# Fixed stack rows filled by DMA, a shifted pass over 66 rows, and a later split of the wide weights

## The chip, the cores and the metric

The kernel runs on one core of a Trainium2 chip. The metric is the device time of one execution in microseconds: 266.58 us before, the median of three runs (266.46 to 270.88). Five engines work beside each other: PE (matrix products, PEld is its weight load), DVE (vector), ACT (activations, copies), POOL (GpSimd) and SP, which here only issues DMAs. DMAs that SP issues go through one queue (q1), those that ACT issues through another (q10). Engines meet only at semaphores.

## The reference

One transformer layer in float32: 4 sequences ("batches") of 256 tokens, width 256, 16 heads of 16, feed-forward width 1024.

```python
x = x + attn(layernorm(x))
x = x + ffn(layernorm(x))

# attn, per batch and head
q, k, v = h @ Wq.T, h @ Wk.T, h @ Wv.T          # rotary embedding on q and k
kf, qf  = elu(k) + 1, elu(q) + 1
lin     = (qf @ (kf.T @ v)) / (qf . sum(kf))    # linear attention
att     = softmax(q @ k.T / 4) @ v
out     = (sigmoid(gate) * lin + (1 - sigmoid(gate)) * att) @ Wo.T

# ffn
out = fwht(silu(h @ W1.T) * (h @ W3.T)) @ W2.T  # fwht: Walsh-Hadamard over 1024
```

## The kernel before

Float32 values are carried as a high and a low part (`_hi`, `_lo`), each rounded to the format that TensorE takes at full rate; a product is the sum of three products of parts. The Hadamard transform is folded into W2 once.

**The stacks.** `q_stack` and `k_stack` are [128, 16 heads, 256 tokens]. For each head, rows 0 to 47 hold q parts (hi, lo, hi) and k parts (hi, hi, lo), 16 rows each, so that one product over the rows gives the three-part product. `scores` (L897) multiplies rows 0 to 63 and DVE takes row maxima (`row_maxima`, L624). The negated maxima then come by DMA into rows 64 and 65 of `q_stack` (`MAXROW` is 64), where `k_stack` holds ones, and `shifted_scores` (L913) multiplies all 128 rows: it gives the score less its row maximum, and ACT takes the exponential (L364). Every other row has to be zero. Rows 0 to 47 are gathered from `parts`, a tensor in DRAM: SP writes the parts there (`write_parts`, L260, four DMAs of 256 KB a batch) and reads them back head by head (`load_stacks`, L271, for each half `c` of the heads six DMAs of 128 KB, each of 16 rows with 8 pieces of 1 KB).

**The order of the work** is written out by hand, one program for each engine. Before the rounds stands a head for batch 0: layer norm (`ln_statistics`, POOL's `rstd` L496, `ln_normalise` L607), transposes on PE (L857), `evac_hT` on ACT (L316), `low_hT` on DVE (L612), the q and k products (L844 to L846), rotary products and sums (L635, L640), the split into parts (`split_parts` L322 on ACT, `first_low_part` L645 on DVE), `write_parts`, `load_stacks`, and the first scores. Beside it ACT and POOL split the wide weights W1 and W3 (`wide_raw`, 128x2048 each) into `w13_hi` (`split_wide`, L408) and `w13_lo` (L539), which the feed-forward reads first in round 1. After the head, round r works on attention of batch r, on projections of batch r+1 and on feed-forward of batches r-1 and r-2.

**Fixed rows.** POOL sets all of `q_stack` to zero (L487) first of all, then computes `rstd` of batch 0, then sets all of `k_stack` to zero (L531) and its rows 64 and 65 to one (L533), and counts `stack_zero` to 2, on which the first `load_stacks` waits.

**SP's order** in the head: x of batch 0, Wq, Wk, x of batch 1, W1, W3; then, once the narrow weights are split, W2 (L248, into the same buffer), x of batches 2 and 3, and Wo (L253, four DMAs of 16 rows); then the four writes of `parts`, and the twelve loads.

Of the kernel before, what the change touches and what calls it, by code (L numbers as in the profile page):

```python
# [48 lines left out]
P = 128  # L49
# [35 lines left out]
def build(nc, x, wqT, wkT, wvT, woT, gate, w1T, w3T, w2T, const, out):  # L85
    with ExitStack() as ctx:
# [7 lines left out]
        def bank(name):  # L94
# [31 lines left out]
        w2_lo = sb("w2_lo", [P, FC, D], F32R)  # L126
        wo = sb("wo", [P, NG, D])
        stats = sb("stats", [P, TT, 6])
        mv = sb("mv", [P, TT, 2])
# [38 lines left out]
        w13_in = [sem("w1_in"), sem("w3_in")]  # L168
        (const_in, w2_in, wo_in, gate_in, mhalf_set, wo_zero, stack_zero, k_zero, v_const, mem_zero, wqkv_hi_s, wqkv_lo_s, w13_hi_s, w1_lo_s, w3_lo_s,
         had_ps, had_sb, fly, w2_hi_s, w2_lo_s, gate_exp, gate_s) = [sem(n) for n in (  # L170
             "const_in w2_in wo_in gate_in mhalf_set wo_zero stack_zero k_zero v_const mem_zero wqkv_hi_s wqkv_lo_s w13_hi_s w1_lo_s w3_lo_s "
             "had_ps had_sb fly w2_hi_s w2_lo_s gate_exp gate_s").split()]
# [63 lines left out]
        def _(sp):  # L236
# [7 lines left out]
            for m, w in enumerate((w1T, w3T)):  # L244
                sp.dma_start(wide_raw[:, m], w.rearrange("(c p) n -> p c n", p=P)).then_inc(w13_in[m], 16)
            sp.wait_ge(wqkv_hi_s, 3)
            sp.wait_ge(wqkv_lo_s, 3)
# [14 lines left out]
            def load_stacks(b, c):  # L262

                sp.wait_ge(parts_out[c], 32 * (b + 1))
                if b == 0:
                    sp.wait_ge(stack_zero, 2)
                else:
                    sp.wait_ge(exp_ps, NH * (b - 1) + HH * (c + 1))
                for m, stack, slots in ((0, q_stack, (0, 1, 0)), (1, k_stack, (0, 0, 1))):
                    for s, half in enumerate(slots):  # L270
                        sp.dma_start(stack[HD * s:HD * s + HD, HH * c:HH * c + HH, :].bitcast(F32),  # L271
                                     parts[b, half, c, m].rearrange("(h d) n -> d h n", d=HD)).then_inc(stack_in[c], 16)
# [29 lines left out]
        def _(act):  # L302
# [116 lines left out]
            evac_hT(0)  # L419
            for m in range(2):  # L420
                split_wide(m)
            for r in ROUNDS:
# [17 lines left out]
                if r >= 0 and has(r + 1):  # L440
                    evac_v(r + 1)
                if r < 0:
                    exp_elu(0)
                    evac_hT(1)
                    evac_hadamard(0)
                    evac_kfT(0)
                    evac_hadamard(1)
                    continue
# [36 lines left out]
        def _(pool):  # L485
            pool.memset(mhalf[:], -0.5).then_inc(mhalf_set, 1)
            pool.memset(q_stack[:].bitcast(F32), 0.0).then_inc(stack_zero, 1)  # L487

# [41 lines left out]
            ln_power(0)  # L530
            pool.memset(k_stack[:].bitcast(F32), 0.0).then_inc(k_zero, 1)  # L531
            pool.wait_ge(k_zero, 1)
            pool.memset(k_stack[MAXROW:MAXROW + 2].bitcast(F32), 1.0).then_inc(stack_zero, 1)  # L533
            pool.wait_ge(stack_zero, 2)
            ln_power(1)
            pool.memset(wo[:], 0.0).then_inc(wo_zero, 1)
            for m, done in enumerate((w1_lo_s, w3_lo_s)):
                pool.wait_ge(w13_hi_s, m + 1)
                pool.tensor_tensor(w13_lo[:, m], wide_raw[:, m], w13_hi[:, m].bitcast(F32), ALU.subtract).then_inc(done, 1)  # L539
# [293 lines left out]
        def _(pe):  # L833
# [74 lines left out]
            def shifted_scores(b, h):  # L908
# [3 lines left out]
                for tt in range(TT):  # L912
                    mm = pe.matmul(bank[:, tt, :], k_stack[:, h, tt * P:tt * P + P], q_stack[:, h, :],  # L913
                                   start=True, stop=True)
# [231 lines left out]
```

## Time and profile before

| What | us |
|---|---|
| Median of three runs | 266.58 |
| Lowest, highest | 266.46, 270.88 |
| Span of the profiled execution, first to last instruction | 262.9 |
| Own device time of the profiled execution | not given by the page |
| Busy: PE, PEld, DVE, ACT, POOL | 215.3, 171.7, 175.3, 97.8, 95.5 |
| First scores of batch 0 start at | 41.87 |

Instruction times are counted from the start of the span. A timeline row gives the start, the length, the engine, the source line and the operation; with xcount over 1 the length is that of the merged run from the first start to the last end. "[a <-b]" is the idle time of the engine before the row and what ended it. The chain of waits is followed back from the last instruction; "issue" in it is time in which the engine named next waited for nothing that the profile shows. A window's DMA share is the mean busy share of the 16 DMA engines.

### The profile page before, as it was taken

Reading aid. Unit: us, or ns where it says so; the run is one execution under the profiler, and the core shown is the slowest. Engines: PE = TensorE matmul, PEld = TensorE weight load, DVE = VectorE, ACT = ScalarE, POOL = GpSimd, SP = SyncE. Lnnn points to the kernel's source line nnn. Section 1 sums busy time; section 2 is a strip of 40 time slices with the busy share of each in tenths; the row PEclk is TensorE's granted clock in tenths of the full one; section 3 lists DMA queues with packets and bytes.
Section 4 is the critical chain, followed back from the end, with each engine's and each line's share of the span. In section 5 each row is a group of like instructions: output and inputs, shape, how many; then the busy total and the mean of one; then the engine's idle time right before and its main releaser. Section 6 shows DMA issues by size and latency. Waiting matters only on the chain.

```text
span 262.9 us, 4040 instructions
## 1 busy us (share of the span) xinstructions
PE 215.3 (82%) x1444; PEld 171.7 (65%) x1444; DVE 175.3 (67%) x340; ACT 97.8 (37%) x196; POOL 95.5 (36%) x73
## 2 busy tenths in 40 slices
PE   0073086887969869999998999999999999986894
PEld 0072056665548558896786788977767896765893
DVE  6958842688886984719869927375997734774532
ACT  2261040043963021468701312688011466612331
POOL 7929400189044364233502461243011224201332
PEclk9999557997999967999999569999999999999999
DMA  7928299031287013005560130026800010000101
GB/s 224 356 59 223 99 177 118 6 134 31 46 101 97 0 40 122 5 1 87 87 70 1 40 122 1 5 59 94 133 0 0 5 42 0 4 0 1 42 1 40
DMA packets 16916, 17.57 MB, mean 67 GB/s; under 512 B 1664, under 2 KB 16256, under 8 KB 16896
## 3 DMA queue, kind: packets, MB, share of 16 engines
q1 hardware_dynamic: 16144, 16.59, 30.1%
q10 hardware_dynamic: 752, 0.73, 0.9%
q8 instruction: 11, 0.18, 0.4%
q14 instruction: 9, 0.07, 0.1%
HBM read 11.93 MB, written 5.24 MB: 65 GB/s over the span
## 4 chain that ended last, share of the span: by engine, by line
PE 48%; issue 21%; DVE 13%; POOL 8%; DMA 6%; SPq 2%; ACT 2%; POOLq 0%; DVEq 0%; ACTq 0%
PE score_bank L897 7%; DMA k_stack<-parts 5%; PE exp_bank L1004 5%; PE score_bank L1004 4%; PE exp_bank L913 4%; DVE rowmax L624 4%; POOL hid_lo L522 4%; PE down_bank L1026 4%; DVE xn L607 4%; PE misc_bank L844 3%; PE misc_bank L963 3%; PE misc_bank L845 2%; PE misc_bank L846 2%; DVE prod L635 2%; PE pv_bank L930 2%
## 5 line engine op out<-in xcount | busy, mean ns | idle before, releaser
L624 DVE TENSOR_REDUCE rowmax<-score_bank 128x2 f32<-128x512 f32 x64 | 43.2, 685 | 30.2 <-PE score_bank L897 30.1
L522 POOL TENSOR_TENSOR hid_lo<-wide_raw,hid_hi 128x256 fp32r<-128x256 f32 x32 | 24.8, 774 | 80.1 <-ACT hid_hi L397 76.6
L364 ACT ACTIVATE prob<-exp_bank 128x512 f32<-128x512 f32 x64 | 37.8, 600 | 14.1 <-PE exp_bank L913 13.8
L897 PE MATMUL score_bank<-k_stack,q_stack 64*128 64x256 f32 x128 | 31.5, 339 | 11.5 <-DVE rowmax L624 7.2
L897 PEld LDWEIGHTS score_bank<-k_stack,q_stack 64*128 64x128 f32 x128 | 19.7, 198 | 23.8 <-DVE rowmax L624 9.1
L913 PE MATMUL exp_bank<-q_stack,k_stack 128*128 128x256 f32 x128 | 28.6, 307 | 1.2 <-ACT prob L364 1.1
L913 PEld LDWEIGHTS exp_bank<-q_stack,k_stack 128*128 128x128 f32 x128 | 19.2, 188 | 12.7 <-issue 8.2
L503 POOL TENSOR_TENSOR roped<-prod 128x512 f32<-128x512 f32 x6 | 7.6, 1269 | 44.8 <-DVE prod L635 44.8
L857 PE MATMUL misc_bank<-cst,xn 128*128 128x128 f32 x16 | 3.4, 352 | 24.2 <-DVE xn L607 24.2
L734 DVE SCALAR_TENSOR_TENSOR wide_raw<-wide_raw,score_bank 128x256 f32<-128x256 f32 x16 | 6.7, 417 | 23.3 <-ACT wide_raw L391 23.3
L1004 PE MATMUL exp_bank<-h2T_hi,w_hi 128*128 128x256 f32 x64 | 19.4, 324 | 0.0
L1026 PE MATMUL down_bank<-w_hi,hid_hi 128*128 128x256 f32 x64 | 17.8, 300 | 1.5 <-ACT hid_hi L397 1.4
L857 PEld LDWEIGHTS misc_bank<-cst,xn 128*128 128x128 f32 x16 | 2.4, 179 | 24.4 <-issue 13.1
L607 DVE TENSOR_SCALAR xn<-xs,mv,rstd 128x256 f32<-128x256 f32 x16 | 12.3, 808 | 8.0 <-POOL rstd L496 7.7
L982 PE MATMUL pv_bank<-wo,att 128*128 128x256 f32 x64 | 16.7, 389 | 1.0 <-DVE att L719 1.0
L1004 PE MATMUL exp_bank<-h2T_hi,w_lo 128*128 128x256 f32 x64 | 17.1, 288 | 0.0
L1004 PE MATMUL score_bank<-h2T_hi,w_hi 128*128 128x256 f32 x64 | 17.0, 289 | 0.0
L1026 PE MATMUL down_bank<-w_lo,hid_hi 128*128 128x256 f32 x64 | 16.7, 282 | 0.0
L1004 PE MATMUL score_bank<-h2T_hi,w_lo 128*128 128x256 f32 x64 | 16.4, 279 | 0.0
L391 ACT ACTIVATE wide_raw<-exp_bank 128x256 f32<-128x256 f32 x16 | 6.2, 384 | 26.3 <-PE exp_bank L1008 24.3
L376 ACT ACTIVATE xs<-pv_bank 128x512 f32<-128x512 f32 x4 | 2.4, 598 | 35.8 <-DVE stats L588 35.8
L930 PE MATMUL pv_bank<-prob,v_strips 128*32 128x256 f32 x192 | 15.3, 391 | 0.1
(116 smaller groups left out, 548.1 us busy)
## 6 DMA issues: line engine op xcount, KB each, us to landing
q_stack<-parts SPq DMA_DIRECT2D x24, 128.0 KB, 4.0
k_stack<-parts SPq DMA_DIRECT2D x24, 128.0 KB, 5.3
parts<-part_hi SPq DMA_DIRECT2D x8, 256.0 KB, 2.2
parts<-part_lo SPq DMA_DIRECT2D x8, 256.0 KB, 3.1
xs<-in_x SPq DMA_DIRECT2D x4, 256.0 KB, 6.5
wide_raw<-in_w1T SPq DMA_DIRECT2D x1, 1024.0 KB, 8.0
wide_raw<-in_w3T SPq DMA_DIRECT2D x1, 1024.0 KB, 10.0
narrow_raw<-in_w2T SPq DMA_DIRECT2D x1, 1024.0 KB, 6.1
```

The lines of the kernel that those rows point to most:

```text
L364: act.activation(prob[:, h % 8], exp_bank[h % 2][:], ACT.Exp, scale=SCALE).then_inc(prob_s, 1)
L522: pool.tensor_tensor(hid_lo[:, n % 3, :], ffn_work[n % 3], hid_hi[:, n % 3, :].bitcast(F32), ALU.subtract).then_inc(hid_lo_s, 1)
L607: dve.tensor_scalar(xn[:, tt, :], xs[:, b, tt, :], mv[:, tt, 0:1], rstd[:, tt:tt + 1], ALU.subtract, ALU.mult).then_inc(ln_xn, 1)
L624: dve.tensor_reduce(rowmax[:, h, :], score_bank[h % 2][:], AX.X, ALU.max).then_inc(rowmax_s, 1)
L844: pe.matmul(out_ap, lhs[0], rhs[0], start=start, stop=False, **kw)
L897: mm = pe.matmul(bank[:, tt, :], q_stack[0:MAXROW, h, tt * P:tt * P + P], k_stack[0:MAXROW, h, :], start=True, stop=True)
L913: mm = pe.matmul(bank[:, tt, :], k_stack[:, h, tt * P:tt * P + P], q_stack[:, h, :], start=True, stop=True)
L930: mm = pe.matmul(bank[STRIP * j:STRIP * j + STRIP, half, :], v_strips[b % 2][:, tt, h, :], prob[:, h % 8, tt, :], start=(tt == 0), stop=(t ...
L963: mm = pe.matmul(bank[:, u, :], mem[:, c, 4 * u:4 * u + 4, :].rearrange("p h e -> p (h e)"), feat[:, c, 0, :], start=True, stop=True)
L982: mm = pe.matmul(bank[:, tt, :], att[:, g, tt * P:tt * P + P], wo[:, g, :], start=False, stop=(g == NG - 1), skip_group_check=True)
L1004: pe.matmul(bank[:, m, :], w[:, m, k, cols], h2T_hi[:, k, :], start=(k == 0 and w is w13_hi), stop=False)
L1026: pe.matmul(bank[:, tt, :], hid_hi[:, n % 3, tt * P:tt * P + P], w[:, c, :], start=(c == 0 and tt == 0 and w is w2_hi), stop=False, skip_g ...
```

## The change

Three parts. (1) POOL no longer writes the stacks: it writes a tile `fill` [128, 2, 256], zeros and ones, and SP issues three DMAs that copy rows of it to the fixed rows: `q_stack` rows 48 to 65 and `k_stack` rows 48 to 63 from zeros, `k_stack` rows 64 and 65 from ones. They stand after W3 and ahead of W2. Rows 66 to 127 are not written any more. (2) `shifted_scores` multiplies rows 0 to 65. (3) ACT's two `split_wide` stand after `split_parts` of batch 0, and POOL's `w13_lo` waits for `feat_s`, the features of batch 0.

```diff
+        fill = sb("fill", [P, 2, S])
...
+            sp.wait_ge(fill_set, 2)
+            for rows, value in ((q_stack[3 * HD:MAXROW + 2], 0), (k_stack[3 * HD:MAXROW], 0), (k_stack[MAXROW:MAXROW + 2], 1)):
+                n = rows.shape[0]
+                sp.dma_start(rows.bitcast(F32), fill[0:n, value, :].unsqueeze(1).broadcast_to([n, NH, S])).then_inc(stack_zero, 16)
             sp.wait_ge(wqkv_hi_s, 3)
...
-                    sp.wait_ge(stack_zero, 2)
+                    sp.wait_ge(stack_zero, 48)
...
             evac_hT(0)
-            for m in range(2):
-                split_wide(m)
...
                 if r < 0:
+                    split_wide(0)
                     exp_elu(0)
                     evac_hT(1)
+                    split_wide(1)
                     evac_hadamard(0)
...
-            pool.memset(q_stack[:].bitcast(F32), 0.0).then_inc(stack_zero, 1)
+            for k in range(2):
+                pool.memset(fill[:, k, :], float(k)).then_inc(fill_set, 1)
...
             ln_power(0)
-            pool.memset(k_stack[:].bitcast(F32), 0.0).then_inc(k_zero, 1)
-            pool.wait_ge(k_zero, 1)
-            pool.memset(k_stack[MAXROW:MAXROW + 2].bitcast(F32), 1.0).then_inc(stack_zero, 1)
-            pool.wait_ge(stack_zero, 2)
             ln_power(1)
             pool.memset(wo[:], 0.0).then_inc(wo_zero, 1)
+            pool.wait_ge(feat_s, 1)
             for m, done in enumerate((w1_lo_s, w3_lo_s)):
...
-                    mm = pe.matmul(bank[:, tt, :], k_stack[:, h, tt * P:tt * P + P], q_stack[:, h, :],
+                    mm = pe.matmul(bank[:, tt, :], k_stack[0:MAXROW + 2, h, tt * P:tt * P + P], q_stack[0:MAXROW + 2, h, :],
```

On SP, from W3's load to the first load of the stacks, the order before was (`narrow_raw<-in_w2T` is W2, `parts<-` are the writes of the parts):

```order
L245 DMA wide_raw<-in_w3T 128x2x1024
L248 DMA narrow_raw<-in_w2T 128x8x256
L250 DMA xs<-in_x 128x2x256 x2
L253 DMA wo<-in_woT 16x4x256 x4
L260 DMA parts<-part_hi 128x2x256
```

and is now:

```order
L246 DMA wide_raw<-in_w3T 128x2x1024
L250 DMA q_stack<-fill 18x16x256
L250 DMA k_stack<-fill 16x16x256
L250 DMA k_stack<-fill 2x16x256
L253 DMA narrow_raw<-in_w2T 128x8x256
L255 DMA xs<-in_x 128x2x256 x2
L258 DMA wo<-in_woT 16x4x256 x4
L265 DMA parts<-part_hi 128x2x256
```

Three DMAs with 576 pieces of 1 KB stand ahead of W2 in the queue; nothing else of SP's order moved.

On ACT, from the split of the narrow weights to the first `evac_hadamard`, the order before was (`w_hi<-wide_raw` is `split_wide`, `prod<-prod` the exponential for the features):

```order
L310 ACTIVATE wqkv_hi<-narrow_raw 128x512 x3
L316 ACTIVATE hT_hi<-misc_bank 128x512
L408 ACTIVATE w_hi<-wide_raw 128x2048 x2
L330 ACTIVATE v_strips<-down_bank 128x32x16
L322 ACTIVATE part_hi<-roped 128x512 x2
L335 ACTIVATE prod<-prod 128x1024
L316 ACTIVATE hT_hi<-misc_bank 128x512
L413 ACTIVATE narrow_raw<-exp_bank 128x512
```

and is now:

```order
L315 ACTIVATE wqkv_hi<-narrow_raw 128x512 x3
L321 ACTIVATE hT_hi<-misc_bank 128x512
L335 ACTIVATE v_strips<-down_bank 128x32x16
L327 ACTIVATE part_hi<-roped 128x512 x2
L413 ACTIVATE w_hi<-wide_raw 128x2048
L340 ACTIVATE prod<-prod 128x1024
L321 ACTIVATE hT_hi<-misc_bank 128x512
L413 ACTIVATE w_hi<-wide_raw 128x2048
L418 ACTIVATE narrow_raw<-exp_bank 128x512
```

The first half of the wide split now stands ahead of the exponential, the second behind the second `hT_hi`.

On POOL, between the first `rstd` and the rotary sums, it was:

```order
L487 MEMSET q_stack 128x4096
L496 ISA
L496 TENSOR_TENSOR rstd<-var_eps,mhalf 128x2
L531 MEMSET k_stack 128x4096
L533 MEMSET k_stack 2x4096
L496 TENSOR_TENSOR rstd<-var_eps,mhalf 128x2
L536 MEMSET wo 128x1024
L539 TENSOR_TENSOR w_lo<-wide_raw,w_hi 128x2048 x2
```

and is now:

```order
L493 MEMSET fill 128x256 x2
L502 ISA
L502 TENSOR_TENSOR rstd<-var_eps,mhalf 128x2 x2
L538 MEMSET wo 128x1024
L542 TENSOR_TENSOR w_lo<-wide_raw,w_hi 128x2048 x2
```

The three large memsets are gone, and `w_lo` keeps its place but has the new wait in front.

## Rows read from the trace of the kernel before

**Rows 1.** The page's first line and its chain, shares of the span by engine

```profile
span 262.9 us, 4040 instructions
...
PE 48%; issue 21%; DVE 13%; POOL 8%; DMA 6%; SPq 2%; ACT 2%; POOLq 0%; DVEq 0%; ACTq 0%
```

**Rows 2.** Chain of waits in order of time: start us, us, what

```profile
21.86 2.78 DVE roped L640
...
31.55 0.70 DVE part_lo L645
...
35.12 6.71 DMA k_stack<-parts
...
41.87 0.74 PE score_bank L897 x4
```

**Rows 3.** Timeline of POOL: start us, us, engine, line, out<-in, xcount

```profile
5.69 3.51 POOL L531 MEMSET k_stack<- 128x4096 f32 x1
9.26 3.54 POOL L533 MEMSET k_stack<- 2x4096 f32 x1
...
19.50 9.48 POOL L539 TENSOR_TENSOR w_lo<-wide_raw,w_hi 128x2048 fp32r<-128x2048 f32 x2
...
72.59 3.27 POOL L528 TENSOR_TENSOR wide_raw<-wide_raw,narrow_raw 128x1024 f32<-128x1024 f32 x1 [6.46 <-DVE narrow_raw L707]
```

**Rows 4.** Timeline of DVE, same columns

```profile
5.79 7.16 DVE L607 TENSOR_SCALAR xn<-xs,mv,rstd 128x256 f32<-128x256 f32 x2 [0.88 <-POOL rstd L496]
...
25.32 4.21 DVE L645 TENSOR_TENSOR part_lo<-roped,part_hi 128x512 fp32r<-128x512 f32 x1
...
30.17 0.69 DVE L640 TENSOR_TENSOR roped<-prod 128x512 f32<-128x512 f32 x1
...
32.16 0.73 DVE L607 TENSOR_SCALAR xn<-xs,mv,rstd 128x256 f32<-128x256 f32 x2
...
34.62 1.23 DVE L656 SCALAR_TENSOR_TENSOR feat<-roped,prod 128x1024 f32<-128x1024 f32 x1 [1.12 <-ACT prod L335]
...
75.18 0.71 DVE L702 TENSOR_TENSOR ginv<-inv,gate 128x16 f32<-128x16 f32 x1
```

**Rows 5.** Timeline of ACT, same columns

```profile
7.32 1.15 ACT L310 ACTIVATE wqkv_hi<-narrow_raw 128x512 fp32r<-128x512 f32 x2 [0.54 <-DMA narrow_raw<-in_wkT]
14.22 0.60 ACT L316 ACTIVATE hT_hi<-misc_bank 128x512 fp32r<-128x512 f32 x1 [5.75 <-PE misc_bank L857]
14.71 3.70 ACT L408 ACTIVATE w_hi<-wide_raw 128x2048 fp32r<-128x2048 f32 x2
```

**Rows 6.** Timeline of SP's DMA issues, same columns

```profile
3.25 0.80 SPq L245 DMA_DIRECT2D wide_raw<-in_w3T  x1
16.83 0.37 SPq L248 DMA_DIRECT2D narrow_raw<-in_w2T  x1
...
25.32 0.39 SPq L260 DMA_DIRECT2D parts<-part_hi  x1
```

**Rows 7.** Windows: stretch, length, busy by engine, granted PE clock, DMA share, GB/s

```profile
10.00:12.40 2.40, 0.00 (x0) 0.00 (x0) 2.40 (x1) 0.00 (x0) 2.40 (x1) 1.00 0.97 387
12.60:17.00 4.40, 2.45 (x10) 2.11 (x11) 3.09 (x7) 2.78 (x3) 0.20 (x1) 1.00 0.00 1
17.80:26.20 8.40, 4.03 (x28) 3.83 (x27) 5.56 (x6) 1.84 (x3) 8.25 (x4) 1.00 0.81 219
26.20:27.40 1.20, 0.00 (x0) 0.00 (x0) 1.20 (x1) 0.00 (x0) 1.20 (x1) 0.54 0.63 219
34.40:46.20 11.80, 8.50 (x36) 6.68 (x34) 4.04 (x9) 2.46 (x5) 0.00 (x0) 0.64 1.12 127
23.20:26.20 3.00, 0.00 (x0) 0.00 (x0) 2.91 (x3) 0.63 (x1) 3.00 (x2) 1.00 0.57 76
```

**Rows 8.** Timeline of PE, the two score passes, same columns as in 3

```profile
57.03 0.73 PE L897 MATMUL score_bank<-k_stack,q_stack 64*128 64x256 f32 x4
...
72.48 0.74 PE L913 MATMUL exp_bank<-q_stack,k_stack 128*128 128x256 f32 x4
```

More of the change, by code:

```diff
@@ L168, in build @@
         w13_in = [sem("w1_in"), sem("w3_in")]
-        (const_in, w2_in, wo_in, gate_in, mhalf_set, wo_zero, stack_zero, k_zero, v_const, mem_zero, wqkv_hi_s, wqkv_lo_s, w13_hi_s, w1_lo_s, w3_lo_s,
+        (const_in, w2_in, wo_in, gate_in, mhalf_set, wo_zero, stack_zero, fill_set, v_const, mem_zero, wqkv_hi_s, wqkv_lo_s, w13_hi_s, w1_lo_s, w3_lo_s,
          had_ps, had_sb, fly, w2_hi_s, w2_lo_s, gate_exp, gate_s) = [sem(n) for n in (
-             "const_in w2_in wo_in gate_in mhalf_set wo_zero stack_zero k_zero v_const mem_zero wqkv_hi_s wqkv_lo_s w13_hi_s w1_lo_s w3_lo_s "
+             "const_in w2_in wo_in gate_in mhalf_set wo_zero stack_zero fill_set v_const mem_zero wqkv_hi_s wqkv_lo_s w13_hi_s w1_lo_s w3_lo_s "
              "had_ps had_sb fly w2_hi_s w2_lo_s gate_exp gate_s").split()]
```

## The prediction

> **What bounds the kernel now.** I read the page first. Its chain is PE for 48% of the span and "issue" for 21% [rows 1]: over most of the run PE is the bound, and the change takes no work from PE there. So I went to the stretch that the change edits, the head up to the first scores, by the chain in order of time. The head is one serial chain: layer norm, transposes, the q and k products, the rotary sums (the first takes 2.78 us), the last `part_lo` at 31.55, the loads of the stacks (the last of the first half issued at 35.12 and landed 6.71 later), and scores at 41.87 [rows 2]. What the head loses, every later round gets back one for one, since nothing behind it waits for anything but the work ahead of it.
>
> Two pieces of it are not work. On DVE two `xn` take 7.16 us where the same two take 0.73 at 32.16 [rows 4]; during the 7.16 POOL clears `k_stack`, 5.69 to 12.80 [rows 3]. And `part_lo` takes 4.21 at 25.32 where such an instruction takes 0.69 to 0.70, the rotary sum 2.78 where the next takes 0.69 [rows 2, 4]; each ends about when one of POOL's two `w_lo` ends (24.2 and 29.0) [rows 3]. DVE is held by POOL's instruction in both places.
>
> **The compute side of the head.** *First piece.* Without the memsets `xn` ends at 5.79 + 0.73 = 6.5, and the transposes after it (1.1) at 7.7. Now ACT's narrow splits are late next: they end at 7.32 + 1.15 = 8.5 [rows 5]. `hT_hi` starts there and not at 14.22: 5.7 us earlier. DVE's `wqkv_lo` fits between. *Second piece.* Without `w_lo` beside them the sum saves 2.78 - 0.69 = 2.1 and the low part 4.21 - 0.69 = 3.5: 5.6 us. The last `part_lo` would start at 31.55 - 5.7 - 5.6 = 20.2 and end at 20.9, 11.3 us earlier. *ACT's moved work.* Each `split_wide` takes 1.9 [rows 5]. The first fits between the second `part_hi` (ends 20.2) and the exponential (22.2), so it costs nothing; the second delays only `kfT`, which is wanted when the scores are. *POOL's moved work.* `w_lo` starts when `feat` ends, 34.62 + 1.23 - 11.3 = 24.6 [rows 4], and takes 9.48 [rows 3]: to 34.1. DVE has two instructions of four columns for the gate in its way. A small one, 16 columns at 75.18, takes 0.71, as long as 512 columns do elsewhere, and ends with POOL's instruction at 75.9 [rows 3, 4]. So I let both wait, the second to 34.1, and the first row maximum of batch 0 can't start before 34.3. POOL's next work (from 51.5) is late enough. *66 rows.* Four matmuls over 64 rows take 0.73, four over 128 rows 0.74 [rows 8]. 66 lies between: zero, at most 0.01 for four, 0.3 us over 128. *`fill`.* Two memsets of 256 columns at 3.51 / 4096 per column [rows 3]: 0.4 us, long done when SP has issued W3 at 4.05 [rows 6].
>
> **The queue side.** This decides. The parts may be ready at 20.9, but their writes stand in SP's queue behind everything issued earlier. Before, the engines were busy to 12.4, idle from 12.6 to 17.0, since W2 was issued only at 16.83, and worked on W2, x and Wo from 17.8 to 26.2; the first write moved from 26.2 [rows 6, 7]. So the queue was clear just when the first parts came. Now:
>
> - W3 is through at 12.5, as before. The fills follow at once: 18, 16 and 2 rows of 16 KB, 590 KB. No fill is in the trace. The nearest row is the stack loads, 1 KB pieces into 16 partitions of the same tiles: 127 GB/s [rows 7], which gives 4.7 us. The ends are the full-width write, 1.20 x 0.63 = 0.76 us for 262 KB, or 1.7 us, and the Wo loads, 76 GB/s, or 7.8 us [rows 7]. I take 4.7, since tile, width and piece are the same: done at 17.2. They fall into the hole that the queue had.
> - W2, x and Wo are now waiting in line. By rate it is 1.57 MB at 387 GB/s, 4.1 us, and Wo's 3.0: 7.1. As traced it is 8.4 [rows 7]. I take 7.7: to 24.9.
> - The four writes of parts, 4 x 0.76 = 3.0: to 27.9. SP needs only the first two landed (26.5) to issue the loads, and first bytes follow an issue by some 0.9 us (25.32 to 26.2, [rows 6, 7]), so the loads follow at 28.0.
> - Before, loads moved from 34.4, and the first half was complete at 41.82 [rows 2, 7]: 7.4 us. Now it is complete at 35.4.
>
> That is 41.8 - 35.4 = 6.4 us, against 11.3 that the engines could give; 34.3 on DVE covers it by a microsecond. After the first scores nothing differs. The granted clock in 34.4 to 46.2 was 0.64 [rows 7], so these products already ran mostly at 1.2 GHz; PE idles longer ahead of them now, and I count nothing either way. The sum against the profiled span is 262.9 - 6.4 = 256.5. The median lies 3.7 above that span; the page gives no own time for the profiled execution, and I let the 3.7 stand: **260.2 us**.
>
> A rule of the Trainium skill bears on the fills. "DMA: Bandwidth & Descriptors", section "Why a DMA increments its semaphore by 16 and not by 1", says that a DMA is spread over the largest number of engines up to 16 that divides its slowest dimension on both sides: 9 engines for 18 rows, 2 for 2 rows. No row of the trace shows such a shape. By it some engines carry more than the mean, which is the second rival below, and the sum would be 263.4 in place of 260.2.
>
> **Rivals.** One: *the fills are cheap.* SBUF to SBUF at the rate of the full-width write, 1.7 us. Then the loads are complete at 32.4 and the gain is 9.4: 257.2. For it: nothing in DRAM is read. Against it: all writes go to 18 partitions, and both traced transfers into 16 partitions were slow. DVE's 34.3 doesn't take it back: PE has products of batch 1 to do after the first two scores, and needs the first maximum only for the third score.
>
> Two: *an uneven split.* If each piece takes an engine what a load's piece took (11.8 us for 96 pieces an engine, 123 ns, [rows 7]) and the 18 rows go to 9 engines, the fullest engine has 32 + 16 + 16 pieces: 7.9 us in place of 4.7. The gain is 3.2: 263.4. Against it: fewer engines on the same rows would disturb each other less than 16 do.
>
> Three, the slower side: *the fills block the queue.* If 18 rows go to two engines only, these have 144 + 16 + 16 pieces, 21.6 us at 123 ns; W2, Wo and the parts wait behind them from 12.5 to 34.1. The first half is then complete at 52.3, 10.5 us later than before: 277.1. It decides against the change once the fills take over 4.7 + 6.4 = 11.1 us. For it: they stand ahead of all that the head still needs. Against it: 16-row loads show no such concentration.
>
> Four: *the engines' gain isn't there*, DVE being slow for another cause than POOL. Then parts come at the old pace and nearly nothing is gained; the pairs 7.16 / 0.73 and 4.21 / 0.69 speak against it. About 266.
>
> **Numbers.** Forecast 0.50 (its own range 258.5 to 262.5: the 7.1 or 8.4 for W2 to Wo, and fills of 3.5 to 6.5 us), cheap fills 0.20, uneven split 0.22, blocked queue 0.05, no gain 0.03. The range 256.8 to 264.5 takes in the first three but their tails. A change under 2%, 5.3 us, counts as none: the border is 261.2. Of the forecast's half some 0.35 lies under it, with the cheap fills 0.55 faster; the rest of the forecast, the uneven split and no gain make 0.40; slower 0.05.
>
> **What would show it.** In the new profile the two first `xn` together under 0.8 us, `hT_hi` of batch 0 at 8.5, no `part_lo` over 0.8, the last one ended by 21. Then the queue: the DMA engines busy without a hole from 12.5 to 40, the fills landed near 17, the writes of parts landing 5 us or more after their issue, first scores near 35.5. If the writes land 2 us after their issue, the queue was not the bound and rival one holds or better; if the fills land at 20, rival two; beyond 23, rival three. I am wrong altogether if the first scores start at 35.5 and the span shrinks by much less than 6: then something behind the head took it back, and I have named nothing for that.

## The result, and the profile after the change

The changed kernel took **269.23 us** (median of 20 runs, 266.88 to 274.26), the kernel before 266.41 beside it (20 runs). By these medians it is slower by 1.1%, or 2.8 us, where 260.2 us and faster were forecast. The executions of one kernel fall into shorter and longer ones, some 4 us apart (shown below); over the shorter ones alone the ratio is 1.0206, with a 95% interval of 1.016 to 1.0252. The sign is clear and the size is 1 to 2%; whether it passes 2% isn't settled.

The page of the kernel after, first line, granted clock in 40 slices, and shares of the chain (as [rows 1]):

```profile
span 265.7 us, 4043 instructions
...
PEclk9995575997555896899999999999999999999999
...
PE 51%; issue 18%; DMA 8%; POOL 7%; DVE 7%; SPq 5%; ACT 2%; POOLq 0%; DVEq 0%; ACTq 0%
```

The same line of the clock in the kernel before:

```profile
PEclk9999557997999967999999569999999999999999
```

The span grew from 262.9 to 265.7, and the slices 10 to 12, counted from 0 (66 to 86 us), are the place to look: three fives, where before has 9, 9 and 9.

**The engines did what was forecast.** DVE in the head (columns as in [rows 4]: start, us, engine and line, tiles, count, and in brackets the idle time before and who ended it):

```profile
5.66 0.74 DVE L610 TENSOR_SCALAR xn<-xs,mv,rstd 128x256 f32<-128x256 f32 x2 [0.88 <-POOL rstd L502]
...
17.04 0.69 DVE L648 TENSOR_TENSOR part_lo<-roped,part_hi 128x512 fp32r<-128x512 f32 x1
...
19.76 0.69 DVE L648 TENSOR_TENSOR part_lo<-roped,part_hi 128x512 fp32r<-128x512 f32 x1 [0.70 <-ACT part_hi L327]
...
24.57 4.09 DVE L750 TENSOR_SCALAR gsum<-gexp 128x4 f32<-128x4 f32 x1
...
28.90 4.22 DVE L754 TENSOR_SCALAR gate<-gate 128x4 f32<-128x4 f32 x1
41.21 1.29 DVE L627 TENSOR_REDUCE rowmax<-score_bank 128x2 f32<-128x512 f32 x2 [8.09 <-PE score_bank L900]
```

ACT and POOL there:

```profile
8.37 0.58 ACT L321 ACTIVATE hT_hi<-misc_bank 128x512 fp32r<-128x512 f32 x1
```

```profile
24.13 8.96 POOL L542 TENSOR_TENSOR w_lo<-wide_raw,w_hi 128x2048 fp32r<-128x2048 f32 x2 [10.50 <-DVE feat L659]
```

The two first `xn` take 0.74 us, `hT_hi` starts at 8.37 (forecast 8.5), no `part_lo` is over 0.69, the last ends at 20.45 (forecast 20.9), and the gate's four-column instructions are held for 4.1 and 4.2 us until `w_lo` is done at 33.1.

**The queue did not.** SP's issues, as [rows 6], and the chain of waits behind them:

```profile
3.80 1.01 SPq L250 DMA_DIRECT2D q_stack<-fill  x1
4.86 1.42 SPq L250 DMA_DIRECT2D k_stack<-fill  x2
...
11.41 8.03 SPq L255 DMA_DIRECT2D xs<-in_x  x2
19.48 2.94 SPq L258 DMA_DIRECT2D wo<-in_woT  x4
22.47 0.43 SPq L265 DMA_DIRECT2D parts<-part_hi  x1
...
25.52 1.36 SPq L265 DMA_DIRECT2D parts<-part_lo  x1
31.78 1.27 SPq L276 DMA_DIRECT2D q_stack<-parts  x3
```

```profile
22.95 8.81 DMA parts<-part_lo
34.03 6.30 DMA k_stack<-parts
40.38 1.22 PE score_bank L900 x4
```

The DMA engines and the clock in three stretches (as [rows 7]):

```profile
26.00:31.80 5.80, 3.76 (x11) 3.12 (x12) 5.73 (x3) 1.20 (x2) 5.80 (x2) 0.50 0.53 164
36.00:40.00 4.00, 0.00 (x0) 0.00 (x0) 0.00 (x0) 0.00 (x0) 0.00 (x0) 0.60 1.16 116
40.00:46.00 6.00, 5.62 (x24) 5.37 (x24) 1.80 (x4) 0.00 (x0) 0.00 (x0) 0.50 0.95 100
```

SP needed 8.03 us to issue two loads of x; before, the same row read 1.10 (at 17.24). The writes of parts, ready from 17.7, were issued at 22.47 and 22.95, and the first two had landed only at 31.76, 8.8 us after the second one's issue. In 26.0 to 31.8 the DMA engines were busy for a 0.53 share on average, against 1.13 in 12 to 24: at the end the landing waited for a remainder; which engines still carried it the window doesn't show.

The fills didn't follow W3, as forecast, but ran beside it. The view of DMAs (KB each, us from issue to landing) has for W3 and W2, now:

```profile
wide_raw<-in_w3T SPq DMA_DIRECT2D x1, 1024.0 KB, 15.5
narrow_raw<-in_w2T SPq DMA_DIRECT2D x1, 1024.0 KB, 17.0
```

and before:

```profile
wide_raw<-in_w3T SPq DMA_DIRECT2D x1, 1024.0 KB, 10.0
narrow_raw<-in_w2T SPq DMA_DIRECT2D x1, 1024.0 KB, 6.1
```

W3, issued ahead of the fills at 3.29, was complete at 18.8 in place of 13.2. The view gives no landing for the fills, but the trace keeps each time at which a DMA raised a semaphore, and on `stack_zero` the last of them is at 23.6 us: the fills were complete there, and not at 17.2.

The scores started at 40.38, 1.5 us earlier than before and 5 later than forecast. PE had then done nothing from 32.7 on, its clock stood at 0.50 (1.2 GHz) through 46, and of the 1.5 us only 0.25 were left at the next scores (46.20 against 46.45), behind the same products.

**Behind the head**, where "nothing differs" was written, PE in batch 0's shifted pass:

```profile
64.35 0.74 PE L916 MATMUL exp_bank<-q_stack,k_stack 66*128 66x256 f32 x4
...
67.86 1.08 PE L933 MATMUL pv_bank<-prob,v_strips 128*32 128x256 f32 x8
```

and before, where the lines are not among the rows above:

```profile
64.42 0.73 PE L913 MATMUL exp_bank<-q_stack,k_stack 128*128 128x256 f32 x4
...
67.72 0.64 PE L930 MATMUL pv_bank<-prob,v_strips 128*32 128x256 f32 x8
```

The first 66-row products at 64.35 take as long as 128-row ones. But from 68 on the same work takes nearly twice as long: `pv_bank`, whose shape the change doesn't touch, 1.08 in place of 0.64. The windows tell why. Before:

```profile
64.00:68.00 4.00, 3.27 (x22) 1.88 (x20) 3.39 (x6) 3.40 (x7) 2.12 (x2) 1.00 0.00 0
68.00:72.00 4.00, 3.99 (x42) 2.27 (x38) 3.69 (x6) 3.92 (x7) 0.00 (x0) 1.00 0.25 60
72.00:76.00 4.00, 3.47 (x33) 1.72 (x34) 3.86 (x7) 3.29 (x7) 3.27 (x1) 1.00 1.17 127
```

After:

```profile
64.00:68.00 4.00, 3.28 (x18) 1.91 (x20) 3.38 (x6) 3.29 (x7) 2.07 (x2) 0.93 0.00 0
68.00:72.00 4.00, 4.00 (x25) 2.15 (x23) 3.69 (x5) 2.66 (x4) 0.00 (x0) 0.50 0.00 0
72.00:76.00 4.00, 4.00 (x25) 1.93 (x24) 2.25 (x3) 2.22 (x5) 3.25 (x1) 0.50 0.97 137
```

In 68 to 72 PE is as busy (3.99 and 4.00 of 4 us), but it gets through 25 products in place of 42: the granted clock is 0.50 in place of 1.00, and it stays there up to 88.

A mark that all kernels have shows where time went: ACT's first instruction of the shifted pass of each batch (`nmT_hi`), and the steps from one to the next, in us. Each row is one profiled execution; the kernels are those of the next section, and "best" is the fastest of them by its median.

| kernel | first scores | batch 0's mark | to batch 1's | to 2's | to 3's | to the end |
|---|---|---|---|---|---|---|
| before | 41.87 | 61.31 | 47.5 | 53.9 | 44.7 | 55.4 |
| after | 40.38 | 61.24 | 54.1 | 50.1 | 44.8 | 55.5 |
| change repeated | 39.69 | 59.84 | 52.8 | 54.0 | 44.8 | 55.5 |
| before, 96 rows | 41.65 | 61.66 | 49.4 | 54.0 | 44.8 | 55.5 |
| before, 66 rows | 41.77 | 62.21 | 54.0 | 53.9 | 44.7 | 55.5 |
| late split | 36.30 | 59.26 | 48.8 | 52.5 | 44.7 | 56.9 |
| late split, 66 rows | 36.40 | 59.38 | 53.7 | 49.8 | 44.7 | 56.2 |
| change, 128 rows | 35.72 | 56.69 | 47.9 | 49.8 | 44.7 | 56.3 |
| best | 30.03 | 49.84 | 49.2 | 49.8 | 44.7 | 56.2 |
| best, 66 rows | 30.14 | 50.06 | 52.7 | 49.7 | 44.7 | 56.4 |

Against before, the profiled execution of the change has -0.1 at the first mark, +6.6 in the step behind it, -3.8 in the next and +0.1 at the end: +2.8, the whole of 265.7 - 262.9. The -3.8 is not the change's own: that step takes 49.7 to 50.2 or 53.9 to 54.0 in nearly every kernel, and the change has once the one and once the other.

### The profile page after: what moved, and what is told of

It reads as the page before. It is cut to its first block, busy times and chain, and to the rows that moved or that the text cites. A ratio compares the mean times of both kernels' runs of the same rounds, so it can differ in the third digit from the quotient of the medians.

```text
span 265.7 us, 4043 instructions
## 1 busy us (share of the span) xinstructions
PE 220.9 (83%) x1444; PEld 174.1 (66%) x1444; DVE 170.4 (64%) x340; ACT 98.0 (37%) x196; POOL 84.9 (32%) x72
## 4 chain that ended last, share of the span: by engine, by line
PE 51%; issue 18%; DMA 8%; POOL 7%; DVE 7%; SPq 5%; ACT 2%; POOLq 0%; DVEq 0%; ACTq 0%
PE score_bank L900 7%; PE exp_bank L916 6%; PE exp_bank L1007 4%; PE pv_bank L933 4%; PE score_bank L1007 4%; POOL hid_lo L528 4%; PE down_bank L1029 3%; DVE rowmax L627 3%; DMA parts<-part_lo 3%; PE misc_bank L966 3%; SPq L255 3%; PE misc_bank L847 3%; DMA k_stack<-parts 2%; DMA narrow_raw<-in_wkT 2%; PE misc_bank L956 2%
## 5 line engine op out<-in xcount | busy, mean ns | idle before, releaser
L528 POOL TENSOR_TENSOR hid_lo<-wide_raw,hid_hi 128x256 fp32r<-128x256 f32 x32 | 24.6, 770 | 76.6 <-ACT hid_hi L402 73.0
L916 PE MATMUL exp_bank<-q_stack,k_stack 66*128 66x256 f32 x128 | 31.3, 334 | 1.0 <-ACT prob L369 1.0
L916 PEld LDWEIGHTS exp_bank<-q_stack,k_stack 66*128 66x128 f32 x128 | 21.2, 209 | 14.8 <-issue 7.4
L933 PE MATMUL pv_bank<-prob,v_strips 128*32 128x256 f32 x192 | 18.0, 452 | 0.0
L985 PE MATMUL pv_bank<-wo,att 128*128 128x256 f32 x64 | 16.7, 389 | 1.0 <-DVE att L722 1.0
L1007 PE MATMUL exp_bank<-h2T_hi,w_lo 128*128 128x256 f32 x64 | 16.7, 284 | 0.0
L327 ACT ACTIVATE part_hi<-roped 128x512 fp32r<-128x512 f32 x8 | 5.0, 630 | 29.0 <-POOL roped L509 26.7
L502 POOL TENSOR_TENSOR rstd<-var_eps,mhalf 128x2 f32<-128x2 f32 x8 | 6.0, 756 | 28.1 <-DVE var_eps L600 27.9
L402 ACT ACTIVATE hid_hi<-wide_raw 128x256 fp32r<-128x256 f32 x32 | 13.3, 415 | 4.3 <-DVE wide_raw L740 4.0
```

The lines of the kernel that those rows point to most:

```text
L402: act.activation(hid_hi[:, n % 3, :], ffn_work[n % 3], ACT.Copy).then_inc(hid_hi_s, 1)
L528: pool.tensor_tensor(hid_lo[:, n % 3, :], ffn_work[n % 3], hid_hi[:, n % 3, :].bitcast(F32), ALU.subtract).then_inc(hid_lo_s, 1)
L916: mm = pe.matmul(bank[:, tt, :], k_stack[0:MAXROW + 2, h, tt * P:tt * P + P], q_stack[0:MAXROW + 2, h, :], start=True, stop=True)
L933: mm = pe.matmul(bank[STRIP * j:STRIP * j + STRIP, half, :], v_strips[b % 2][:, tt, h, :], prob[:, h % 8, tt, :], start=(tt == 0), stop=(t ...
L985: mm = pe.matmul(bank[:, tt, :], att[:, g, tt * P:tt * P + P], wo[:, g, :], start=False, stop=(g == NG - 1), skip_group_check=True)
L1007: pe.matmul(bank[:, m, :], w[:, m, k, cols], h2T_hi[:, k, :], start=(k == 0 and w is w13_hi), stop=False)
```

## The experiments

Ratios are to the kernel before beside it; intervals are 95%. "Median" is over all runs of that kernel, with the median of before in brackets. My theory after the result had two parts: 66 rows cost PE its clock in batch 0's shifted pass, and the fills cost the queue what the engines gained. The rivals were that one of them alone did it, or that the late split did.

### What each part does alone

**Only 66 rows**, and **96 rows**:

```diff
-mm = pe.matmul(bank[:, tt, :], k_stack[:, h, ...], q_stack[:, h, :], ...)
+mm = pe.matmul(bank[:, tt, :], k_stack[0:MAXROW + 2, h, ...], q_stack[0:MAXROW + 2, h, :], ...)   # rows66
+mm = pe.matmul(bank[:, tt, :], k_stack[0:MAXROW + 32, h, ...], q_stack[0:MAXROW + 32, h, :], ...)  # rows96
```

> The kernel before with one edit: the shifted pass multiplies rows 0 to 65 in place of all 128; the other rows are zero, so nothing is left out. Rows theory (the chip grants the lower clock in a stretch where PE multiplies 66 rows and has little else): in batch 0 the shifted pass, which has no feed-forward work beside it, runs at a granted clock near 0.5 from about 68 us on, the first scores of batch 1 come near 82 us in place of 78.25, and the time is 3 to 6 us above before. Timing theory (in the changed kernel the clock fell because the pass came in another phase after another head; the rows play no part): batch 0's pass keeps a clock of 1.0 as before and the time stays within 1 us of before.

> The kernel before with the shifted pass over rows 0 to 95. A dose test of the rows theory. If what counts is the number of rows fed to PE, 96 lies between 66 and 128: the clock falls for part of batch 0's pass or not at all, and the time is 0 to 4 us above before. Timing theory: as before, within 1 us.

66 rows: 1.0275 [1.0225, 1.0325], median 271.02 (265.4). 96 rows: 1.0058 [1.0001, 1.0116], median 267.59, 2.2 us over. Windows with 66 rows:

```profile
64.00:68.00 4.00, 3.72 (x12) 2.65 (x11) 3.39 (x6) 2.50 (x5) 3.04 (x2) 0.50 0.02 4
```

and with 96:

```profile
64.00:68.00 4.00, 3.54 (x14) 2.23 (x12) 3.39 (x6) 2.68 (x7) 2.17 (x2) 0.74 0.00 0
68.00:72.00 4.00, 3.99 (x38) 2.28 (x38) 3.70 (x6) 3.92 (x7) 0.00 (x0) 1.00 0.11 33
```

The head is unchanged in both (41.77 and 41.65). With 66 rows the clock is at 0.50 from 64 to 88 and batch 0's step takes 54.0 in place of 47.5; with 96 it is 0.74 in 64 to 68, 1.00 in 68 to 76 and 0.61 in 80 to 84, and the step takes 49.4. So the number of rows alone brings it about, without the fills and with the old order, and it is worth 5.6 us by the medians. The rows that are left out hold zeros: that they hold nothing does not make them worthless for the clock.

**Only the late split**, then **with 66 rows**:

```diff
 evac_hT(0)
-for m in range(2):
-    split_wide(m)
 ...
+    split_wide(0)
     exp_elu(0)
     evac_hT(1)
+    split_wide(1)
 ...
 pool.memset(wo[:], 0.0).then_inc(wo_zero, 1)
+pool.wait_ge(feat_s, 1)
```

> The kernel before with only the wide split moved late (ACT and POOL, as in the change); POOL's memsets and 128 rows stay. Each piece of the head on its own: the first xn still takes 7.2 us, part_lo and the rotary sum take 0.69 each, the last part_lo ends at 26.6. W2 is still issued at 16.8, so the queue is clear at 26.2 and the writes of the parts start there. First scores at 36 to 37.5 in place of 41.87, and the time 3 to 6 us under before. If only the sum of all parts brings anything (rival), the first scores stay above 40 and the time within 1 us of before.

> The kernel late_split (before with only the wide split moved late, 257.3) with the shifted pass over 66 rows and nothing else: all of the change but the fills. Rows theory: the granted clock is 0.5 through batch 0's shifted pass, and the time is 4 to 7 us over late_split: 261 to 264.5. What then lies between this and the changed kernel is the price of the fills in SP's queue, less the 6 us that POOL's memsets hold xn: 3 to 7 us. If rows play no part: 257 to 258.5.

Late split alone: **0.9689** [0.964, 0.9738], median 257.25 (265.51). With 66 rows: 1.0023 [0.9978, 1.0068], median 263.09 (264.72). The memsets still hold `xn` for 7.16 us, but parts are ready at 26.9 in place of 32.2, and the queue takes them at once: first scores 36.30, 5.6 earlier, just the 5.6 worked out for this piece. The time fell by 8.3 us, more than the 3 to 6 expected. 66 rows take 5.8 of the 8.3 us back. The profiled execution of the late split was its slowest (263.9 us, span 262.1), so its head is read from it and not its later steps. In the head it has 2.1 us at batch 0's mark; with a short step to batch 2's mark (4.1) that makes 6 of the 8.3 us, and where the rest comes from no trace of a typical run shows. The mark came 2.1 us earlier, and not 5.6. Two things stand between it and the scores: the clock was 0.50 from 48 to 64, with 66 rows too, where before had 1.00 up to 60, and the first maximum waits (below). How they share the 3.5 us isn't shown. DVE in the late split, the cover that I had at a microsecond:

```profile
35.39 4.24 DVE L752 TENSOR_SCALAR gate<-gate 128x4 f32<-128x4 f32 x1
39.54 1.27 DVE L625 TENSOR_REDUCE rowmax<-score_bank 128x2 f32<-128x512 f32 x2
```

Here the gate's wait does hold the first maximum: the scores are there at 36.30, the maximum starts at 39.54. What that costs this version wasn't tried.

**The change, with the wide split in its old place**, run twice, and **the change once more** beside it:

```diff
 evac_hT(0)
+for m in range(2):
+    split_wide(m)
 ...
-    split_wide(0)
     exp_elu(0)
     evac_hT(1)
-    split_wide(1)
 ...
-pool.wait_ge(feat_s, 1)
```

> The changed kernel with the wide split back in its old place: fills and 66 rows, without the third part. hT_hi is still early (8.4), ACT's two w_hi follow it at 13.3, when W3 has landed, so POOL's w_lo runs from about 15 to 25 and holds the rotary sums and low parts again: the last part_lo ends near 26 to 28. By then the queue, held by the 18-row fill, is nearly clear (31.8 for the first writes' landing in the changed kernel), so the head loses little against the changed kernel: first scores at 40 to 42.5 and time 268 to 272. If the late split is what costs in the change (rival), this kernel is 2 us and more faster than the change.

> The kernel fill_old_split (fills, 66 rows, wide split in its old place) beside the changed kernel on the same chip. Late split costs: 1.5% or more under the changed kernel, first scores no later than its. Chip and hour only: within 1% of it.

> The changed kernel once more, beside its relatives on one chip. It was 2.1% over before when measured alone; its relative with the old wide split (fill_old_split) was level with before on another chip. If the late split costs in the company of the fills, this kernel is 1.5% or more over that relative here too: 268 to 270 against 265 to 266.5. If the two differ by the chip and the hour only, both lie within 1% of each other.

Old place: 0.9984 [0.995, 1.0019] and 1.0111 [1.0038, 1.0185], medians 265.54 (266.11) and 265.77 (264.72). The change again: 1.0211 [1.0133, 1.0289], median 268.74. The first run's issues:

```profile
11.31 5.95 SPq L255 DMA_DIRECT2D xs<-in_x  x2
...
26.25 0.36 SPq L265 DMA_DIRECT2D parts<-part_lo  x1
31.46 1.27 SPq L276 DMA_DIRECT2D q_stack<-parts  x3
```

The parts are ready 5.8 us later than in the change (the last `part_lo` starts at 25.53, not 19.76), and yet the stack loads are issued at 31.46, not 31.78, and the scores start at 40.04, not 40.38. **Beside the fills the late split, worth 8 us by itself, gains nothing: the writes wait for the DMA engines and not for DVE.** In the second run of it the scores start at 37.99, against 39.69 in the repeated change. The expected 268 to 272 us did not come: by the medians the change is 3.7 and 3.0 us slower than this version, so that the rival, that the late split costs beside the fills, fits the first pair. In the second the ratios differ by 1.0%, between what either side had asked for, and their intervals overlap. The spans of its two profiled executions differ by 3.7 us: 1.4 at the first mark, -1.1 in the next step, 4.2 by a long step against a short one (see below) and -0.8 at the end. Whether the change has the long step more often isn't shown, and the cause stays open.

### The fills

**18 rows as 16 and 2**; then **16 rows only, and the ones of k behind Wo** (the two rows of q get the maximum later anyway; both kernels have 66 rows):

```diff
-for rows, value in ((q_stack[3 * HD:MAXROW + 2], 0), (k_stack[3 * HD:MAXROW], 0), (k_stack[MAXROW:MAXROW + 2], 1)):
+for rows, value in ((q_stack[3 * HD:MAXROW], 0), (q_stack[MAXROW:MAXROW + 2], 0), (k_stack[3 * HD:MAXROW], 0), (k_stack[MAXROW:MAXROW + 2], 1)):   # q16_2
+fill_rows(q_stack[3 * HD:MAXROW], 0)           # ones_late
+fill_rows(k_stack[3 * HD:MAXROW], 0)
 ... (W2, x, Wo)
+fill_rows(k_stack[MAXROW:MAXROW + 2], 1)
 ... (ahead of the first load of the stacks)
-sp.wait_ge(stack_zero, 48)
+sp.wait_ge(stack_zero, 64)                     # q16_2 only: four fills
```

> The changed kernel with one edit: the fill of the 18 rows of q_stack is issued as two DMAs, of 16 and of 2 rows. The bytes and the rows are the same, the shifted pass stays at 66 rows. Uneven split theory (18 rows are carried by fewer DMA engines, so those lag, hold SP's issue of x and the landing of everything behind): SP issues the two x loads in about 4 us in place of 8.03, the first scores come at 35.5 to 37 in place of 40.4, and the time is 2 to 5 us under the changed kernel, 264 to 267, with the clock still at 0.5 in batch 0's shifted pass. Bytes theory (590 KB into few rows take this long however they are cut): SP's issue still takes about 8 us, the first scores stay near 40.4 and the time near 269.

> The changed kernel with both odd shapes out of the way: q_stack gets only its 16 rows 48 to 63 (rows 64 and 65 are overwritten by the maxima anyway), and the 2 rows of ones go behind Wo. The shifted pass stays at 66 rows. This is the kernel after128 but for the number of rows and POOL's two memsets. Split theory: SP's two x issues take about 4 us, the first scores come at 35 to 36.5 (after128: 35.72; q fill in 16 + 2 rows: 37.91; change: 40.38). Rows theory: the granted clock is 0.5 through batch 0's shifted pass again, first scores of batch 1 near 77.5 to 79 in place of after128's 74.0, and the time is 3 to 7 us above the 257 of after128's undisturbed runs: 261 to 265. If the rows play no part, it equals after128 within 1 us.

Ratios 1.0032 [0.9999, 1.0065] and 1.0038 [0.9959, 1.0117], medians 266.56 (265.51) and 267.07 (266.11). SP with 16 and 2:

```profile
11.86 6.10 SPq L255 DMA_DIRECT2D xs<-in_x  x2
```

x takes 6.10 us to issue in place of 8.03, and with the ones late as well 4.08; first scores 37.91 and 37.76. Neither comes as early as expected (37 and 36.5 at the latest), and the second one's time is above its 261 to 265 us. One execution each can't give a price of the shape at the first scores either: with the fills of 18, 16 and 2 rows as they are, the same issue took 8.03 and 6.42 us in the change and 5.95 and 4.76 with the wide split in its old place, and the first scores came between 37.99 and 40.38. In time the shape does count: the change has 1.0206 and 1.0211, these two 1.0032 and 1.0038, and the intervals don't meet. By the medians that is some 2 us.

"DMA: Bandwidth & Descriptors" of the Trainium skill, section "Why a DMA increments its semaphore by 16 and not by 1", gives 18 rows 9 engines and 16 rows 16. The trace agrees. By that section a DMA on fewer than 16 engines raises its semaphore once for each of them and once, at its issue, for the rest, so 18, 16 and 2 rows make 10 + 16 + 3 = 29 increments. `stack_zero` has 29 in the change, two of them at 5.2 and 6.7 us, right behind the issues, and the other 27 from 16.7 on; it has 38 with rows of 16, 2, 16 and 2, and 35 with 16, 16 and 2.

**x and Wo behind the stack loads:**

```diff
-for b in range(2, NB): sp.dma_start(xs[:, b], ...)
-(the wait for wo_zero and the four Wo loads)
 ...
         load_stacks(r + 1, c)
+    if r < 0: (the same x and Wo loads)
```

> The changed kernel with the loads of x of batches 2 and 3 and of Wo moved on SP behind the loads of the stacks of batch 0 (66 rows as in the change). Queue theory (the head is bound by what stands in SP's queue ahead of the writes of the parts, and by SP being held while it issues them): x and Wo take some 4 to 5 us out of the line, the first scores come 4 to 6 us earlier, at 34.5 to 36.5 in place of 40.4, and the time falls by 3 to 6 us. Rival (the fills themselves or the loads' own rate hold the head): first scores stay within 1.5 us of 40.4 and the time within 1.5 us of the changed kernel.

0.9971 [0.9923, 1.002], median 263.93 (265.4). Parts are issued as soon as they are ready (17.31, the last at 20.75), the loads at 26.23, first scores 34.76. That is 7.1 us of head, yet at most 1% in time: in the profiled executions 5.9 us are left at the first mark, and the step behind it, with 66 rows, is 6.4 us longer than before. This kernel also gives the plainest price of the fills, beside the last one of the next part, in which POOL's memsets set both stacks and all else is the same: the first two writes, issued at 17.3 and 18.0 here and 17.2 and 17.9 there, land at 26.2 and at 20.1, the first scores come at 34.76 and 30.14, and the ratios are 0.9971 and 0.9769.

**The change with 128 rows**, rows 64 to 127 of both stacks set by POOL, ones late:

```diff
-(the three fills)
+fill_rows(q_stack[3 * HD:MAXROW], 0)
+fill_rows(k_stack[3 * HD:MAXROW], 0)
 ... (W2, x, Wo)
+sp.wait_ge(k_zero, 1)
+fill_rows(k_stack[MAXROW:MAXROW + 2], 1)
 ... (ahead of the first load of the stacks)
 sp.wait_ge(stack_zero, 48)
+sp.wait_ge(k_zero, 2)
 ... (POOL, behind the memset of wo)
+pool.memset(k_stack[MAXROW:P].bitcast(F32), 0.0).then_inc(k_zero, 1)
+pool.memset(q_stack[MAXROW:P].bitcast(F32), 0.0).then_inc(k_zero, 1)
 ... (PE)
-mm = pe.matmul(..., k_stack[0:MAXROW + 2, h, ...], q_stack[0:MAXROW + 2, h, :], ...)
+mm = pe.matmul(..., k_stack[:, h, ...], q_stack[:, h, :], ...)
```

> The changed kernel with the shifted pass over all 128 rows again. Rows 64 to 127 are set to zero by POOL in its idle time before the late wide split (2 memsets of 3.5 us), the ones go to rows 64 and 65 of k_stack by the same DMA after Wo. Rows theory: batch 0's pass keeps a clock of 1.0, first scores of batch 1 near 77 to 78 us, and the time is 3 to 5 us under the changed kernel: 264 to 266.5, about as before. Timing theory: the clock falls at 68 us all the same, and the time stays at 269.

**0.9734** [0.9658, 0.9809]; by the medians 261.37 (265.4), 0.985. Two of its six executions took 256.3 and 257.2 us, the other four 261.2 to 262.5; the profiled one, with a span of 255.4, is one of the two.

```profile
11.44 4.03 SPq L259 DMA_DIRECT2D xs<-in_x  x2
```

```profile
35.72 1.22 PE L912 MATMUL score_bank<-k_stack,q_stack 64*128 64x256 f32 x4 [8.37 <-DMA k_stack<-parts]
```

```profile
68.00:72.00 4.00, 3.48 (x33) 2.13 (x30) 3.81 (x6) 2.91 (x7) 3.26 (x1) 1.00 1.17 120
```

The scores start at 35.72, where the forecast had 35.4, the clock is 1.00 in the pass, and the span is 255.4 where the forecast had 256.5 (of the 7.5 us under before 4.6 come by the earlier first mark and 4.1 by the short step, see below; the other steps take 1.3 back). With 16-row fills and 128 rows the forecast's head comes about in this execution; the kernel above with the same fills and 66 rows had its scores at 37.76, and no row that I read shows why. Between these two the rows are again worth 3.1% by the ratios, 5.7 us by the medians.

### Is there a version that beats both?

The memsets are not the trouble in themselves, only their place before `xn`. **Late split, `k_stack` cleared once the first `xn` is done**, no fills, 128 rows; then **x and Wo behind the stack loads as above**; then **that with the gate's instructions ahead of the rotary products**; then **that second one with 66 rows**.

```diff
 ln_power(0)
+pool.wait_ge(ln_xn, TT)
 pool.memset(k_stack[:].bitcast(F32), 0.0).then_inc(k_zero, 1)
```

```diff
 low_hT(1)
-gate_weights()
 ...
 ln_statistics(1)
+gate_weights()
 rope_product(0, 0)
```

> The kernel before with the wide split moved late and the two memsets of k_stack moved behind batch 0's xn on POOL; no fills, 128 rows. Engine side as in the changed kernel, queue without the fills' 590 KB and still with x and Wo ahead of the writes. Queue theory: the queue works on W2, x and Wo from 12.5 to about 20.2, the writes to 23.3, and the loads land near 30.7 to 31.5; DVE is held by the late w_lo until 33, so the first row maximum comes at 33. The time is 8 to 11 us under before, 254.5 to 257.5, less up to 2 us if the clock is low longer. If POOL's memsets hold DVE's wqkv_lo too (rival), these take 3 us and more and the head gains 3 us less.

> As mem_late, and x of batches 2 and 3 and Wo are issued behind the loads of the stacks. Queue theory: writes of the parts start when they are ready, 17.5, and loads land near 29.5 to 30.5; but DVE is held until 33 by the late w_lo, and PE runs only two scores ahead. Within 1.5 us of mem_late, in front by at most that. Rival (queue bound up to here): 2 us or more under mem_late.

> The fastest kernel so far (memsets behind xn, wide split late, x and Wo behind the stack loads, 128 rows) with DVE's three small gate instructions moved ahead of the rotary products, where DVE waits for PE and POOL is not in a two-input operation. The first row maximum now follows the first scores (30.0) at 30.9 in place of 33.1. Lock theory (DVE was held to 33.1 by the two w_lo through these small instructions): the rounds start up to 2 us earlier and the time falls by 1 to 2 us, to 250 to 251. Rival: PE's products of batch 1 pace this stretch, and the maxima are early enough: within 0.7 us.

> The kernel mem_x_late (251.8) with the shifted pass over 66 rows. The rows theory in a third surrounding, with the head 10 us shorter. Clock 0.5 through batch 0's shifted pass, and 4 to 7 us over mem_x_late: 256 to 259. If the rows play no part: within 1 us of 251.8.

| kernel | ratio | interval | median (before) | first scores | first row maximum |
|---|---|---|---|---|---|
| memset behind `xn` | 0.9531 | 0.948 to 0.9583 | 253.21 (265.51) | 32.12 | 34.38 |
| and x, Wo late | **0.946** | 0.9407 to 0.9513 | **251.83** (265.51) | 30.03 | 33.13 |
| and gate early | 0.9487 | 0.9437 to 0.9537 | 252.01 (266.11) | 29.84 | 30.67 |
| x, Wo late, 66 rows | 0.9769 | 0.9704 to 0.9834 | 256.19 (264.72) | 30.14 | 33.19 |

DVE with the memset behind `xn`:

```profile
5.76 0.73 DVE L609 TENSOR_SCALAR xn<-xs,mv,rstd 128x256 f32<-128x256 f32 x2 [0.88 <-POOL rstd L496]
...
9.92 1.28 DVE L760 TENSOR_TENSOR wqkv_lo<-narrow_raw,wqkv_hi 128x512 fp32r<-128x512 f32 x2
...
12.11 1.54 DVE L599 TENSOR_SCALAR var_eps<-mv 128x2 f32<-128x2 f32 x1
```

`xn` takes 0.73, now that POOL clears `k_stack` only behind it (6.55 to 13.6). `wqkv_lo` stands beside the memset and takes 1.28 for two, as before (at 15.46): it isn't held. The small `var_eps` is, from 12.11 until the memset ends, and that costs nothing, since the second batch's `rstd` has time. The memset behind `xn` brings 12.3 us where 8 to 11 were expected. The best version is 14 us under before: in the profiled executions 11.5 at batch 0's mark, -1.7 in the next step, 4.1 by the short one and -0.8 at the end, 13.1 of span. Freeing DVE of the gate's wait brings the first maximum 2.5 us forward and no time at all: the rival that PE has other work until then holds once x and Wo are late. 66 rows cost this version 4.4 us. With the pair above that makes four with the same answer: 5.6, 5.8, 5.7 and 4.4 us by the medians, 2.75% to 3.4% by the ratios. Only the first was taken beside its partner; in the others each kernel was compared with before at its own hour.

### The step that is short or long

In 145 to 155 us, before:

```profile
145.00:150.00 5.00, 4.86 (x19) 3.68 (x20) 4.83 (x10) 1.58 (x4) 1.52 (x3) 0.58 0.15 52
150.00:155.00 5.00, 5.00 (x22) 4.55 (x22) 1.53 (x3) 0.82 (x2) 5.00 (x4) 0.50 0.45 151
```

after:

```profile
145.00:150.00 5.00, 5.00 (x28) 3.80 (x28) 4.60 (x12) 0.42 (x1) 0.61 (x1) 1.00 0.00 0
150.00:155.00 5.00, 3.24 (x19) 2.27 (x18) 4.97 (x10) 1.19 (x3) 2.46 (x3) 1.00 0.16 54
```

Batch 1's step is long (53.9) where the clock falls there and short (50.1) where it doesn't. The repeated change had 0.50 in 150 to 160 and a step of 54.0. It happens with 66 and with 128 rows, and between executions of one kernel, so 4 us of any one profiled comparison are luck. The first mark doesn't decide it: the change with ones late had it at 58.15 and a long step, the wide split in its old place at 60.47 and a short one. What tips it wasn't tried.

## Why the prediction was wrong, step by step

- **The engines: right.** 8.37 for 8.5, 20.45 for 20.9, w_lo 24.13 to 33.1 for 24.6 to 34.1.
- **"Zero, at most 0.01 for four" for 66 rows: the step that cost most.** The durations were compared at one clock, and there they are equal still (0.74 and 0.73). That the clock might answer to the rows wasn't asked. It is 6.6 us in the profiled step and 4.4 to 5.8 by the medians of four pairs. The forecast's last sentence named the case ("something behind the head took it back") and had no mechanism and no chance for it, and the slower side had 0.05.
- **The fills at 4.7 us behind W3, everything behind them at its old price: the second.** W3 was to be through at 12.5 and the fills at 17.2; they ran beside each other and were complete at 18.8 and 23.6. The first two writes were to be there at 26.5 and landed at 31.76. The loads of the head end 5.0 us later than forecast (40.4, not 35.4). Rival two, the uneven split, put them at 38.6, 1.8 us short; that 18 rows go to 9 engines is shown, and that this is the whole of the delay is not, since 16-row fills also left the first two writes 7.5 to 8.1 us on their way. By the prediction's own sign, fills landing beyond 23, rival three would hold, but its two engines for 18 rows and its 52.3 us did not come. By medians the fills in place of the memsets turn 263.09 (late split, 66 rows) into 268.74 beside it, 5.6 us, although they free `xn`; with x and Wo out of the way they cost 4.6 us at the first scores (34.76 and 30.14).
- **"What the head loses, every later round gets back one for one": not so.** With the late split alone 5.6 us at the first scores were 2.1 at batch 0's mark, in the change 1.5 were 0.1, and what stands behind the mark moves by 4 us either way with the clock.
- **"I count nothing either way" for the clock after a longer idle time: wrong by 1.4 us.** The same products took 5.8 us from the first scores to the next in place of 4.6, and 1.4 were gone at the mark. They ran at 0.50 until 46, where before had 0.84 in 42 to 44 (four score products 1.22 us, before 0.74).
- **"The median lies 3.7 above that span, and I let it stand":** the profiled execution after took 267.52 with a span of 265.7, so 1.8 lie around a span; the other 1.9 were the spread of before.

The sum in terms of the profiled executions: 256.5 forecast + 4.9 (6.4 of head, 1.5 came) + 1.4 (cold start of the scores) + 6.6 (rows) - 3.8 (the step that is short or long, which is luck) + 0.1 = 265.7. By medians, taking the parts one on the other: late split -8.3, 66 rows +5.8, fills +5.6, together +3.1 where 2.8 was measured. That they agree is no confirmation: the three differences share their ends and add up to the repeated change (268.74) less before at the late split's hour (265.51). Less the before beside it (264.72) it is 4.0.

## What to carry to other kernels

Equal durations at one clock don't make a smaller matmul free: look at the granted clock of the stretch where it runs, and try the smaller shape alone. A DMA put into a hole of the queue is paid by what stands behind it, on the issuing engine as well as on the DMA engines; judge its shape (how many rows) and not only its bytes. And when an instruction holds another engine, moving it a microsecond can be worth more than replacing it: the best version kept both memsets.

## What was not expected of the hardware

- The granted clock falls from 1.00 to 0.50 within a pass in which PE stays as busy (3.99 and 4.00 of 4 us in 68 to 72), when its products have 66 rows in place of 128; with 96 it is 0.74 and 0.61 in two of the windows of 4 us and 0.97 to 1.00 in those between. In later batches, the steps show no such loss (44.7 and 55.4 before, 44.7 and 55.5 with 66 rows). There feed-forward products of 128 rows stand between; that these are the reason wasn't tried.
- Fills from a small tile delay SP's own issuing: two loads behind fills of 18, 16 and 2 rows took 8.03 and 6.42 us in the change, 5.95 and 4.76 with the wide split in its old place, 6.10 behind fills of 16, 2, 16 and 2, and 4.03 and 4.08 behind two of 16. The place of these loads, right behind W3 and W2, is not the reason: without fills, in the version with the memset behind `xn`, they stand there too and take as long as before:

```profile
11.70 1.10 SPq L250 DMA_DIRECT2D xs<-in_x  x2
```

- A four-column instruction on DVE is held as long as a whole POOL instruction takes: 4.09 to 4.24 us, where the same `gsum` took 0.16 with the wide split in its old place.
